# Two-layer AdaLN block (Mamba-2 and expert layers): VectorE's order inside layer zero's experts

## The reference

```python
h = layernorm(x) * (1 + ca) + sa
x = x + ga * L0_attn(h)      # Mamba-2 scan: 32 heads of 128, state 128
h = layernorm(x) * (1 + cb) + sb
x = x + gb * L0_ffn(h)       # 8 experts of 128 hidden columns, best 2 by sigmoid score, and one shared expert
h = layernorm(x) * (1 + ca) + sa
x = x + ga * L1_attn(h)      # 128 heads, 32 largest and 32 smallest keys of each
h = layernorm(x) * (1 + cb) + sb
x = x + gb * L1_ffn(h)       # 8 experts of 176 columns and a shared one
```

```python
r = s[e] * xf
out += (silu(r @ w1[e].T) * (r @ w3[e].T)) @ w2[e].T
```

## Time and profile before

| what | value |
|---|---|
| median of 3 runs | 949.82 us (946.18, 949.82, 950.10) |
| profiled execution | 950.15 us |
| its span in the trace | 948.2 us |
| TensorE matmul busy | 835.6 us (88%) |
| VectorE busy | 783.8 us (83%) |
| ScalarE busy | 555.5 us (59%) |
| GpSimd busy | 463.0 us (49%) |
| mean granted TensorE clock | 0.966 of full speed |

### The profile page before, as it was taken

How to read it: one execution, slowest core, us unless ns; L and a number is a source line. 1 busy time by engine, 2 the same in 40 slices (tenths; PEclk the granted TensorE clock), 3 DMA queues, 4 the chain that set the end, 5 groups by cost and what they waited for, 6 DMA issues and landing times. The chain is left out here.

```text
span 948.2 us, 16734 instructions
## 1 busy us (share of the span) xinstructions
PE 835.6 (88%) x5486; PEld 586.1 (62%) x5486; DVE 783.8 (83%) x1749; ACT 555.5 (59%) x1225; POOL 463.0 (49%) x459
## 2 busy tenths in 40 slices
PE   4768899999999999999999889999988675688897
PEld 3546677667777777777777667765555523345565
DVE  6978899999999999999988898787759968856752
ACT  3657787777777877778776566511116382552321
POOL 2146576586577654545444435545223222424642
PEclk9989999999999999999999899999999887999999
DMA  7113433443343332221332233152211413302122
GB/s 266 29 36 104 139 97 126 134 113 123 123 139 117 125 96 71 90 90 45 135 89 90 49 93 83 36 182 90 79 45 50 86 16 53 145 0 68 56 91 78
DMA packets 52662, 87.16 MB, mean 92 GB/s; under 512 B 5824, under 2 KB 23744, under 8 KB 51808
## 3 DMA queue, kind: packets, MB, share of 16 engines
q1 hardware_dynamic: 43360, 73.50, 26.1%
q10 hardware_dynamic: 9216, 12.59, 3.6%
HBM read 70.67 MB, written 15.40 MB: 91 GB/s over the span
## 5 line engine op out<-in xcount | busy, mean ns | idle before, releaser
L616 PE MATMUL bank<-hTs,wA 128*128 128x512 bf16 x768 | 179.9, 382 | 0.8 <-DVE u L1869 0.8
L2448 POOL TENSOR_TENSOR xbuf<-xbuf,dec 128x384 f32<-128x384 f32 x64 | 53.4, 834 | 214.9 <-ACT xbuf L1337 169.5
L1869 DVE SCALAR_TENSOR_TENSOR u<-bank,chn,u 128x511 f32<-128x511 f32 (+2 forms) x192 | 142.9, 744 | 3.5
L616 PEld LDWEIGHTS bank<-hTs,wA 128*128 128x128 bf16 x768 | 75.5, 99 | 83.8 <-issue 5.6
L688 PE MATMUL bank<-wB,yb 128*128 128x256 f32 x512 | 121.1, 380 | 0.7 <-DVE acc L1825 0.7
L688 PEld LDWEIGHTS bank<-wB,yb 128*128 128x128 f32 x512 | 92.5, 190 | 11.2 <-issue 1.1
L767 PE MATMUL bank<-Mm,xbuf 128*128 128x128 f32 x512 | 72.3, 286 | 20.3 <-DVE yv L1896 19.1
L2458 POOL TENSOR_TENSOR yb<-yv,gs 128x512 f32<-128x512 f32 x64 | 81.7, 1276 | 15.6 <-DVE yv L1896 15.4
L767 PEld LDWEIGHTS bank<-Mm,xbuf 128*128 128x128 f32 x512 | 66.1, 196 | 31.9 <-issue 25.0
L1347 ACT ACTIVATE rel<-csb,cs 128x128 f32<-128x128 f32 x256 | 82.5, 417 | 0.0
L1337 ACT ACTIVATE xbuf<-bank,dtv 128x128 f32<-128x128 f32 x256 | 73.0, 373 | 12.7 <-PE bank L733 12.7
(11 more groups left out here) (278 smaller groups left out, 1838.5 us busy)
## 6 DMA issues: line engine op xcount, KB each, us to landing
csb<-csd SPq DMA_DIRECT2D x64, 256.0 KB, 3.5
wA<-in_win SPq DMA_DIRECT2D x32, 256.0 KB, 4.4
wAd<-wA ACTq DMA_DIRECT2D x32, 256.0 KB, 4.5
wA<-wAd SPq DMA_DIRECT2D x32, 256.0 KB, 3.8
wB<-in_wob SPq DMA_DIRECT2D x8, 512.0 KB, 6.0
wBd<-wB ACTq DMA_DIRECT2D x32, 128.0 KB, 4.4
wB<-wBd SPq DMA_DIRECT2D x8, 512.0 KB, 5.5
sS<-cbd SPq DMA_DIRECT2D x16, 256.0 KB, 3.3
```

Source lines behind the costliest of these rows:

```text
L616: last = nc.tensor.matmul(out, wpart(a, kt), hpart(c, kt), start=n == 0, stop=n == 5)
L1869: nc.vector.scalar_tensor_tensor(out=u[:, n % 2, d:S], in0=bank[0][:, 0:S - d], scalar=chn[:, hid, 3 - d:4 - d], in1=u[:, n % 2, d:S], op0 ...
```

## The change

For every tile VectorE now does this tile's multiplication first, then the next tile's weighing, then the pieces of the normalisations. In layer one the order stays as it was, since `ahead` is false there and its pieces stand behind the multiplication already.

```diff
                 for m in range(B * nf):
                     ahead = L == 0 and m + 1 < B * nf and tile(0, m + 1)[1] >= SHARED[0]
-                    shared = tile(L, m)[1] < SHARED[L]
-                    if ahead and not shared:
+                    hidden(m)
+                    if L == 0 and m == 0:
+                        gated_rows(1)
+                    if ahead:
                         scaled(m + 1)
                     if L == 0:
                         first_batch(m)
-                    hidden(m)
-                    if L == 0 and m == 0:
-                        gated_rows(1)
-                    if ahead and shared:
-                        scaled(m + 1)
                     (heads_ended if L else second_batch)(m)
                     if m == last_tile(L, 0) + 2:
                         add_experts(0)
```

## The result

The changed kernel takes 943.92 us, the median of 20 runs (938.58 to 948.10), against 949.96 us for the kernel before in as many runs (944.60 to 958.85). The ratio is 0.9937 with a 95% interval from 0.9920 to 0.9953: 6.0 us less, between 4.5 and 7.6. The forecast was 943.0 us with a range from 939.3 to 947.5.

What follows compares the result with a forecast made beforehand. The prediction saw TensorE waiting for GpSimd's split, which waits for VectorE's multiplication, placed late in VectorE's order. Gains of 3.4 + 0.7 + 2.8 = 6.9 us from 950.15 gave 943.2, stated as 943.0 us, range 939.3 to 947.5.

Steps and rivals of the forecast that it cites:

- The chain: Layer zero's experts: the multiplication stood behind the next tile's weighing, which waits for its products; the new order loses 3.95 us.
- The late tiles: Tiles 10 to 17: waits behind `add_experts(0)` and the pieces of statistics and roots go, 0.7 us gained.
- the clearing: Between products(10) and products(17): a part of the 28.93 us that is no wait, at most 0.59 us.
- The end: From products(17) to the transposes: 11.01 us become 8.19, a gain of 2.8 us.
- The early tiles: Tiles 1 to 9: earlier multiplications and splits let TensorE reach products(10) 3.4 us sooner.
- the step at rows out(7): Tiles 4 to 9: TensorE's only remaining idle there, 0.17 us before rows out(7), goes.
- The clock: TensorE at rows out(2): an unknown cost, 1.3 us lost if the clock halves again behind the shorter wait.
- The cover: VectorE's standing for silu, 0.84 us a tile if uncovered, is hidden behind TensorE's period with 1.3 us to spare.
- its first matmuls start on transposed rows: Start of layer one: argument against Nothing, since these rows hang directly on TensorE's queue; no size given.
- Half: Rival: early tiles give little, only the end and late tiles gain, 3.5 us, time 946.3; chance 0.16.
- Nothing: Rival: the stage ends earlier, but layer one waits for something else or the clock loses it, 949.5 us; chance 0.10.
- Slower by the port: Rival: batch 0's earlier multiplications are blocked by GpSimd's subtraction and split, 959.6 us; chance 0.08.

Runs made afterwards that it cites:

- three part experiments: The kernel before with the new order only at tiles 1 to 8, 9 to 15, or 16 and 17; ratios 0.998, 1.0011 and 0.9974.
- first part experiment: The kernel before with the new order only at tiles 1 to 8; ratio 0.998 (0.9949 to 1.0011).
- port experiment: The changed kernel with two more GpSimd subtractions 128x384 per tile at tiles 1 to 5; products(1) to products(10) 42.2 us, time not compared over several runs.

## Why the prediction was right

**The chain.** It held to the row. The multiplications stand before the weighings, the three waits that were to remain remained (forecast about 0.6, 1 to 1.5 and 1 to 1.5 us; found 0.52, 1.10 and 1.54), and the three part experiments landed within 0.1 us of the expected distances, which were by then read from the changed kernel's profile.

**The terms.** Of 6.9 us, 7.7 were found in the stage. The late tiles were put 0.15 too low (0.85): the clearing was taken at 0.59 us, and from its start to the next rows out it costs 0.43. The end was put 0.2 too high (2.63), since the last split took 1.15 us, not 1.04. The early tiles were put 0.8 too low. Two terms were mis-sized there: the root steps, where the forecast let GpSimd block longer (multiplication(2) came 13.50 us after products(1), the forecast had 13.88), and the normalised rows, taken at 2.9 us and measured at 2.41. With them the wait for split(3) vanished. Also the step at rows out(7) was worth 0.34, not 0.17: without the wait, the transposed weights cost 0.44 us.

**The clock.** That it would hold behind the shorter wait was a choice without a row behind it, and half of the gain between rows out(1) and rows out(3) hung on it. It held in all four profiles of the new order, so it was no luck of one run; but why 1.10 us is short enough, when 2.26 us once passed and 1.58 us once did not, no run here shows. The experiment with filled idle time priced it at 1.3 us in the old order, as the forecast had bounded it. At the end there was luck in the number: the forecast counted from the 11.01 us of the only profile that it had, and three other profiles of the old end have over 0.4 us more.

**The cover.** VectorE's standing for silu costs nothing where TensorE has a period of work; so it was. The forecast that its waits for silu would rise to about twelve was wrong. They are four under silu's name and two under rows out's, 7.7 us, and two of 0.15 us under VectorE's own (at 678.78 and 682.13). At the other tiles a piece filled the gap, or nearly.

**The end of the stage.** The step "its first matmuls start on transposed rows" was right but not the whole. Two chains leave the stage, 0.17 us apart, and both begin at the split of the last tile. The change moved what they share, so the gain arrived; a change to one of them did not pay.

**Half, nothing, slower.** Half falls with the distances of the first part experiment (4.2 us in the early tiles, though not with its timing), and with the time of the change: 3.5 us less lies outside its interval, 4.5 to 7.6. Nothing falls with the timing. Slower by the port falls by the sixteen multiplications at 0.69 us; meetings came only with added GpSimd work. The small step of 1.03 us, which the forecast took as a sign for this rival, has one tensor input (L1659, a tensor_scalar) and is no row of the multiplication's kind; the first such rows are those of the port experiment. The timed gain, 6.0 us, is 1.7 less than the stage's 7.7, which lies at the edge of its interval. Whether something behind the stage takes back a part or it is the spread of the runs stays open; the span's 0.55 lies within what that stretch varies by.

## What to carry to other kernels

In an engine's hand-written order, put first what another engine is waiting for and whose inputs are ready, then what waits for a third engine, then the work nobody awaits: with the same instructions the order was worth 6 us here, and one swap of the last two made the kernel slower than at the start. Where a pipeline has a tile of slack, follow the chain from one tile's inputs to its consumer and count how many other tiles' waits stand in it. Before moving the end of a stage, look for the second chain that leaves it.

## What the runs showed of the hardware

- In the experts of layer zero and right behind them, a lower granted clock followed holes in TensorE's work of 2.00 us (0.57, 0.59 and 0.64 in three kernels, while rows out(2) ran), 2.33 to 2.70 us before the old rows out(16) (0.51 to 0.70 in four kernels, while they ran), 2.42 us (0.79 in 693.4 to 698.0), 2.67 us (0.60 in 637.1 to 641.4), 2.69 us (0.69 and 0.62 in the two windows behind it) and 1.58 us (0.50). It stayed at 1.00 behind 1.10, 1.11 and 1.54 us, and once behind 2.26 us. So a longer hole was mostly the worse one, but its length alone does not tell what follows. A hole's price can thus be more than its length: 1.3 us on top of 2.0 in one case, 0.9 on top in another.
- A VectorE step of 128x4 elements that takes 0.16 us took 1.03 us when it met a GpSimd subtraction of 1.04 us. In the kernel with the weighing last, where such steps stand behind the multiplication that releases the subtraction, one of them took 0.82 to 1.03 us at each of the tiles 13 to 16.
- GpSimd is held as well: a subtraction of 0.82 us that began 0.05 us after a multiplication with two SBUF inputs took 1.34 us, and the multiplication kept its 0.69.
